# A mixture-of-experts audio block: three instead of four tiles in the part of the output that TensorE joins last

## What is computed

```python
h = tokenise(x)                                  # 896 rows of 128
h = h + attention(layernorm(h))
x = layernorm(h)
y  = sum over the 2 chosen of 10 experts: gate * (elu(x @ e_w1 + e_b1) @ e_w2 + e_b2)
sh = conv(silu(conv(x, sh_w1, 9 taps) + sh_b1), sh_w2, 1 tap) + sh_b2
z = x + y + sh
out = h + (z - mean(z)) * rsqrt(var(z) + 1e-5) * ln_g + ln_b
```

## Time and profile before

| | us |
|---|---|
| median of 3 runs | 159.66 |
| lowest and highest | 159.06, 160.29 |
| profiled execution | 159.7 |
| its span | 157.8 |

### The profile page before, as it was taken

The page is one execution under the profiler, slowest core; times in us unless marked ns, Lnnn a source line. Parts: engine busy times, 40 slices in busy tenths (PEclk is TensorE's granted clock), DMA queues, the critical chain, the costliest instruction groups (busy, mean ns, idle before and its releaser), DMA issues.

```text
span 157.8 us, 3057 instructions
## 1 busy us (share of the span) xinstructions
PE 145.6 (92%) x998; PEld 131.6 (83%) x998; DVE 129.4 (82%) x356; ACT 75.7 (48%) x201; POOL 87.7 (56%) x79
## 2 busy tenths in 40 slices
PE   7799879999998999999999988999999999999950
PEld 2599669999985747899999958999999999979830
DVE  0087999999998989879977765999999999895871
ACT  2223965201018769971043424677777777741030
POOL 3063899999999984004777720056464454470230
PEclk9999999999999999999999999999999999999999
DMA  5999999992980000000399229999899985004304
GB/s 150 262 395 412 295 201 277 209 123 50 199 150 2 2 0 4 0 0 0 64 334 324 93 73 287 391 386 360 308 320 283 355 296 198 34 33 130 124 0 116
DMA packets 19619, 28.57 MB, mean 181 GB/s; under 512 B 4838, under 2 KB 14182, under 8 KB 19604
## 3 DMA queue, kind: packets, MB, share of 16 engines
q1 hardware_dynamic: 16984, 21.69, 44.5%
q0 software_dynamic: 1696, 5.52, 14.6%
q10 hardware_dynamic: 924, 1.17, 2.8%
HBM read 19.94 MB, written 5.28 MB: 160 GB/s over the span
## 4 chain that ended last, share of the span: by engine, by line
PE 64%; POOL 13%; DVE 7%; DMA 7%; issue 4%; ACT 2%; SPq 0%; DVEq 0%; POOLq 0%
PE psum L629 14%; PE psum L746 13%; PE psum L760 12%; POOL xs_rows L501 9%; DMA xT_s<-xT 4%; PE psum L858 4%; POOL prod L351 4%; PE psum L718 3%; PE psum L537 3%; PE psum L733 2%; PE psum L560 2%; DVE stats L1153 2%; DMA xs_rows<-xT_s,slot 1%; DMA xb<-xs_rows 1%; PE psum L549 1%
## 5 line engine op out<-in xcount | busy, mean ns | idle before, releaser
L511 POOL DMA_INDIRECT ys_rows<-yb,xid x22 | 21.1, 961 | 24.9 <-ACT yb L1109 24.9
L1099 ACT ACTIVATE wu<-psum,wring 128x128 f32<-128x128 f32 x92 | 26.1, 373 | 11.2 <-PE psum L746 11.2
L1408 DVE SCALAR_TENSOR_TENSOR tb<-psum,wring,wu 128x128 f32<-128x128 f32 x92 | 25.9, 344 | 0.8
L760 PE MATMUL psum<-wring,tb 128*128 128x128 f32 x184 | 24.6, 276 | 0.2 <-DVE tb L1408 0.2
L746 PE MATMUL psum<-xTb,wring 128*128 128x128 f32 x184 | 24.3, 275 | 0.0
L501 POOL DMA_INDIRECT xs_rows<-xT_s,slot x14 | 14.4, 1027 | 16.1 <-DVE slot L1340 12.1
L760 PEld LDWEIGHTS psum<-wring,tb 128*128 128x128 f32 x184 | 22.4, 192 | 1.1 <-DVE tb L1408 1.0
L629 PE MATMUL psum<-prod,ident_s 128*128 128x196 f32 (+1 forms) x120 | 21.6, 341 | 1.1 <-POOL prod L351 1.1
L746 PEld LDWEIGHTS psum<-xTb,wring 128*128 128x128 f32 x184 | 22.4, 192 | 0.0
L629 PEld LDWEIGHTS psum<-prod,ident_s 128*128 128x128 f32 x120 | 21.1, 190 | 1.2 <-issue 1.2
L363 POOL TENSOR_TENSOR prod<-es,vt 128x3136 f32<-128x3136 f32 x3 | 19.4, 6479 | 0.2 <-ACT es L979 0.2
(11 more groups left out here) (185 smaller groups left out, 276.8 us busy)
## 6 DMA issues: line engine op xcount, KB each, us to landing
wring<-wexp SPq DMA_DIRECT2D x23, 514.0 KB, 4.9
wu<-raw POOLq DMA_DIRECT2D x2, 1536.0 KB, 11.6
raw<-wsh SPq DMA_DIRECT2D x2, 768.0 KB, 9.1
xs_rows<-zero_s SPq DMA_DIRECT2D x1, 1472.0 KB, 16.2
ys_rows<-zero_s SPq DMA_DIRECT2D x1, 896.0 KB, 17.7
xT_s<-xT SPq DMA_DIRECT2D x2, 384.0 KB, 6.0
wu<-wsh SPq DMA_DIRECT2D x1, 768.0 KB, 7.3
xb<-xs_rows SPq DMA_DIRECT2D x1, 585.0 KB, 6.2
```

Source lines behind the costliest of these rows:

```text
L511: pool.indirect_dma_start(ys_dram, bass.IndirectOffsetOnAxis(ap=xid[:, j:j + 1], axis=0), yb[:, j % NY, :], None)\
L760: ins = mm(y_ps(j), tb[:, j % NTT, c, :], wring[:, j % NR, W2 + c * P:W2 + (c + 1) * P], start=(c == 0), stop=(c == HC - 1))
L1099: ins = A(eb[:, j % NEB, c, :], ps[U_BANKS[j % NU]][:, c * P:(c + 1) * P], ACT.Exp, bias=wring[:, j % NR, B1 + c:B1 + c + 1])
L1408: ins = V.scalar_tensor_tensor(tb[:, j % NTT, c, :], ps[U_BANKS[j % NU]][:, c * P:(c + 1) * P], wring[:, j % NR, B1 + c:B1 + c + 1], eb[:, ...
```

## The change

Tile 3 moves from part 0 to part 1. Part 0, whose fetched rows TensorE adds and which ends last, has tiles 0 to 2; part 1, which VectorE joins first, has tiles 3 to 6. GpSimd's powers of part 0 are taken for two tiles and one, and of part 1 for four. Part 1 has a fourth diagonal now, at columns 384 to 511 of xnT, where the joined rows of tile 3 lie; a wait ahead of it holds it until VectorE has read those rows in less_mean.

```diff
-HALVES = [(0, 512), (512, N)]
+HALVES = [(0, 384), (384, N)]
...
-TILES = [range(0, 4), range(4, NT)]
+TILES = [range(0, 3), range(3, NT)]
...
-R_PARTS = [[range(0, 2), range(2, 4)], [range(4, NT)]]
-TILE_RANGE = [slice(0, 4), slice(4, NT)]
+R_PARTS = [[range(0, 2), range(2, 3)], [range(3, NT)]]
+TILE_RANGE = [slice(0, 3), slice(3, NT)]
...
             for n, i in enumerate(TILES[1]):
+                if n == TILES[1][0]:
+                    act.wait_ge(S("scaled_mean"), NT + 1)
                 A(xnT[:, n * P:(n + 1) * P], ident_s[:], ACT.Copy, scale=rstd[:, 3, i:i + 1])\
                     .then_inc(S("diag_done"), 1)
```

## The result

The changed kernel takes 161.42 us (median of 22 runs, 160.28 to 162.58), the kernel before in the same comparison 159.95 (22 runs). The ratio is 1.0094, with a 95% interval of 1.0076 to 1.0112: about 1.5 us slower. The forecast was 160.1, within 159.2 to 160.9, so the time lies outside the range. The forecast had also taken about 1% as the least that a measurement tells from no change; the interval shows that 0.9% was enough. The profiled execution took 161.18 with a span of 159.4, 1.6 more than before's.

A forecast was written before the change was run, and what follows sets the result against it. The prediction took TensorE, 64% of the span, as the bound before the last stage. VectorE came out level; the stores' drain added 0.4 us, giving 157.8 + 0.4 = 158.2 of span and 159.7 + 0.4 = 160.1 us, range 159.2 to 160.9.

The forecast's parts named there:

- A: TensorE's shared_down ahead of the first block_up: two more matmul records, exposed, cost 0.22 us (bounds 0 and 0.22).
- B: TensorE's second_bias: 512 and 384 columns swapped; the first one's saving is hidden, the second pays 0.21 us.
- C: TensorE's shared_down(1): three more tile products of two records each, 0.67 us before bank 1 is complete.
- D: TensorE's last_block(1): two more records, 0.22 us before bank 1 is complete.
- signs of being right: First L746 0.2 later, join 1.3 later without fetch wait, no bank 0 wait, last row near 154.6, stores 0.5 apart.
- one of being wrong: Signs against the forecast: VectorE still waiting for TensorE, a last result past 155, or stores over 0.8 us apart.
- first rival: Final stores: the two pairs don't hinder each other, span ends at 157.7, time 159.6 us; chance 0.25.
- the second: Rival on the final stores: writes at 197 GB/s or below, second pair waits for the first, 160.5 us; chance 0.15.
- covered by the later start: VectorE's joins: the 0.37 us wait for the fetched rows disappears because the first join starts later.
- third rival: Fetch of expert rows: 256 KB per queue lands late, VectorE stops 0.5 us at the joins, 160.6 us; chance 0.1.
- the forecast's 0.4: End of the kernel: the close store pairs drain until 157.4 instead of 157.0, moving the end by +0.4 us.
- four tiles' waiting is turned into work, no more: VectorE in the last stage: its 1.21 us wait for bank 0 is filled with work, and it comes out level.

## Why the prediction was wrong

**TensorE's steps were right within 0.1.** A was to be 0.22. The first L746 load starts at 96.29 after 96.10, 0.19 later, of which 0.06 is block_x behind a later xb; the last blocks run 0.19 later as well (L760 at 141.25 after 141.06), so A was worth 0.13 to 0.19. B, C and D brought the first join to 146.83; forecast 146.85.

**VectorE's own work was right.** The joins take 0.69 (forecast 0.69), the power of four tiles 1.07 (1.12), the pair and the single tile together 1.22 (1.2), the fourth diagonal 0.30. The new statistics start right behind less_mean, and the wait for bank 0 is gone. VectorE ends at 155.66 and ScalarE at 155.44, 0.2 apart, where the forecast had them 0.3 apart. One of the forecast's signs of being right failed, since the second join waits for the fetch, and one of being wrong showed, since the last result ends past 155.

**The stores were right in sum.** The forecast had 3.9 us from the first pair's issue to the end of the span (154.27 to 158.2); it is 159.4 - 155.46 = 3.9 in the changed kernel and 157.2 - 153.36 = 3.8 with three warm-ups less. The stores' data ran from 156.66 to 158.60, 1.9 us as forecast. The first rival had 3.4 and the second 4.3. The drain of 1.05 us that the first rival quotes comes from a figure for DMAs issued by GpSimd, while these stores go out on SP's and ScalarE's queues; no trace shows it.

**The step that failed is the wait for the fetched rows.** The forecast put it at nothing, "covered by the later start"; it was 1.20 us at the second join. The third rival did price it, but with "Issued at 143.40 + 0.22 = 143.62". The issue was at 145.21 in the changed kernel, and at 145.67 and 145.68 in its further profiles, 1.6 to 2.1 later. The rest of that rival's mechanism came true: VectorE stops, at the second join and not the third, has no slack left, and the end moves by the same amount, 1.1 us from 147.6 to 148.72. With the forecast's 0.4 that is the 1.5 us measured. But the rival priced the landing (3.4 after the issue, less than the 4.0 assumed) and took the issue as fixed by the scatter. What the forecast had overlooked is that the last scatter's landing depends on what else the DMA engines carry, and that includes instruction packets, which stand in the same trace: in before the packet is at 146.7, where the scatter has long landed.

The statement "four tiles' waiting is turned into work, no more" was wrong in the same place. The 1.21 us that VectorE waited for bank 0 were not idle time to be filled: they hid the joins' dependence on the fetch. Before with 24 matmuls more spends 1.03 of them on the late fetch and loses nothing measurable; the changed kernel has already spent them.

Without the late fetch the profiles agree with the forecast's +0.4: from before's first trace the rest grows from 18.59 to 18.67 to 18.79, and A puts up to 0.2 ahead of it. That is a comparison with one trace; the rest of before spreads from 18.50 to 19.24. Of the times, the interval with fetches that depend on nothing (0.9958 to 1.0021) ends just short of those 0.4 us (1.0025), and the one with 60 matmuls more (0.9993 to 1.0038) holds both 0.4 us and nothing. The 1.0077 of the kernel with three warm-ups less stays unexplained.

## What to carry to other kernels

- An idle time that an engine spends waiting for the last of several inputs also covers the lateness of all the others. Before filling it, list what else arrives in that time and by how much each could be late. The price of the change is set by the one that now comes last, and the range has to reach that far.
- Look at the instruction packets in the trace beside each small DMA on which the end depends. A change in the number of instructions, even at the far end of an engine's program, can put one beside it: here four small matmuls did. Before a difference of a per cent between two such variants is put down to the change itself, compare the packet's place in both.
- Where a loss appears that no term explains, a fixed input in place of the awaited data, and a few useless instructions in a place that waits anyway, tell a dependence from an alignment. Take more than one count of the useless instructions: here 60 more gave a clear answer, 24 more half of one, and three fewer a profile and times that don't agree.

## What the runs showed of the hardware

- The instruction packets of 16 KB on queue 8, eight in each execution, took 0.9 to 1.5 us where they were the last. When one ran beside the last scatter of 128 rows, the scatter's last 4 KB piece started within 0.02 us of the packet's end, in eight executions of eighteen; the fetch that waits for the scatter went out 1.1 to 1.2 us after the packet's end, up to 2.1 later than the usual 2.29 from the scatter's issue.
- That these packets are TensorE's code is inferred from what moves them: 60 small matmuls at TensorE's start, in place of six of its warm-up matmuls, moved the first from 18.0 to 11.6 and the last from 143.0 to 137.8. But the last one doesn't follow the count smoothly. In before one or two matmuls more left it at 145.6 to 146.3, four put it at 142.0, and 24 left it at 142.5. What sets these two places, and why the change's two records were enough to bring it to 143.0 when two small matmuls in before were not, stays open; the change also moves TensorE's waits, and that was not tried apart.
- A store's issue took 0.57 and 0.83 us on SP's queue with the pairs close together, against 0.50 and 0.57 there before; on ScalarE's it was 0.53 and 0.60 against 0.49 and 0.53. The stores' data started some 1.2 us after the first issue, as forecast.
